# A decoder layer on one core: experts of the first token half in native fp32 beside attention and SSM of the second

## Time and profile before

| | us |
|---|---|
| median of 3 runs | 541.66 |
| lowest, highest | 541.35, 547.73 |
| span of the profiled execution | 542.0 |
| PE busy | 417.3 (77%) |
| DVE busy | 397.2 (73%) |
| ACT busy | 230.3 (42%) |
| POOL busy | 161.0 (30%) |

### The profile page before, as it was taken

The page is one execution under the profiler, slowest core; times in us unless marked ns, Lnnn a source line. Parts: engine busy times, 40 slices in busy tenths (PEclk is TensorE's granted clock), DMA queues, the critical chain, the costliest instruction groups (busy, mean ns, idle before and its releaser), DMA issues.

```text
span 542.0 us, 18523 instructions
## 1 busy us (share of the span) xinstructions
PE 417.3 (77%) x8258; PEld 299.6 (55%) x8258; DVE 397.2 (73%) x542; ACT 230.3 (42%) x434; POOL 161.0 (30%) x118
## 2 busy tenths in 40 slices
PE   1987357887666859867746778749999996999994
PEld 0634146554554445554444443427888875888883
DVE  0545925999989996899984899988785885846434
ACT  1485284553550435544422344304646532344430
POOL 2000743000001000000000000315888875589861
PEclk9996666659867777866676897869999997999998
DMA  8112510250331132211122121510233222323201
GB/s 251 66 24 70 160 24 4 81 133 11 62 96 47 42 96 65 80 42 43 42 81 81 43 79 41 156 46 22 62 86 88 63 74 79 98 79 96 79 1 39
DMA packets 23434, 38.37 MB, mean 71 GB/s; under 512 B 4657, under 2 KB 7483, under 8 KB 23355
## 3 DMA queue, kind: packets, MB, share of 16 engines
q1 hardware_dynamic: 23195, 37.15, 24.3%
q0 software_dynamic: 160, 0.04, 0.1%
HBM read 35.93 MB, written 1.25 MB: 69 GB/s over the span
## 4 chain that ended last, share of the span: by engine, by line
PE 47%; DVE 35%; issue 11%; ACT 4%; DMA 1%; SPq 1%; DVEq 0%; ACTq 0%
PE bank L793 10%; DVE arena_h L1396 8%; PE bank L782 7%; DVE arena_h L1401 4%; PE bank L997 4%; PE bank L998 4%; PE bank L1001 4%; DVE arena_h L1390 4%; PE bank L977 4%; PE bank L978 4%; PE bank L979 4%; PE bank L983 2%; DMA xT<-in_x_t 1%; PE bank L811 1%; DVE u L1351 1%
## 5 line engine op out<-in xcount | busy, mean ns | idle before, releaser
L782 PE MATMUL bank<-arena_h,const 128*128 128x512 f32 x128 | 85.3, 808 | 10.3 <-DVEq L1402 10.2
L719 POOL TENSOR_TENSOR hg_lo<-vkp,hg_hi 128x512 fp32r<-128x512 f32 x50 | 67.8, 1359 | 40.5 <-DVE hg_hi L1617 40.5
L715 POOL TENSOR_TENSOR w_ring<-w_raw,w_ring 128x512 fp32r<-128x512 f32 x16 | 24.2, 1520 | 179.9 <-ACT w_ring L1254 179.9
L1396 DVE TENSOR_TENSOR_SCAN arena_h<-arena_s,arena_h 128x1024 f32<-128x1024 f32 x32 | 73.2, 2288 | 2.9 <-ACT arena_s L1114 1.8
L793 PE MATMUL bank<-vkp,tiles 32*32 32x32 f32 (+1 forms) x3072 | 40.0, 205 | 35.0 <-issue 23.3
L1261 ACT ACTIVATE vkp<-bank,b 128x512 f32<-128x512 f32 x50 | 34.5, 689 | 72.4 <-POOL hg_lo L719 52.0
L1617 DVE CAST hg_hi<-vkp 128x512 fp32r<-128x512 f32 x50 | 33.7, 676 | 38.0 <-PE bank L1001 34.7
L793 PEld LDWEIGHTS bank<-vkp,tiles 32*32 32x32 f32 x3072 | 36.7, 124 | 40.1 <-issue 26.9
L1114 ACT ACTIVATE arena_s<-delta,negA 128x510 f32<-128x510 f32 x64 | 43.1, 713 | 36.8 <-DVEq L1397 36.3
L793 PE MATMUL bank<-qke,tiles 32*32 32x48 f32 (+1 forms) x1984 | 35.3, 233 | 23.5 <-issue 16.7
L782 PEld LDWEIGHTS bank<-arena_h,const 128*128 128x128 f32 x128 | 29.1, 247 | 39.9 <-issue 25.9
(11 more groups left out here) (175 smaller groups left out, 902.3 us busy)
## 6 DMA issues: line engine op xcount, KB each, us to landing
bc<-scr_x SPq DMA_DIRECT2D x32, 512.0 KB, 4.9
raw_ahead<-in_w SPq DMA_DIRECT2D x26, 256.0 KB, 2.7
w_raw<-in_w SPq DMA_DIRECT2D x24, 256.0 KB, 2.7
xT<-in_x_t SPq DMA_DIRECT2D x1, 1024.0 KB, 7.7
xres<-in_x_tok SPq DMA_DIRECT2D x1, 1024.0 KB, 9.7
beta_kc<-scr_b SPq DMA_DIRECT2D x32, 32.0 KB, 1.8
out<-xres SPq DMA_DIRECT2D x8, 128.0 KB, 1.8
wqkvb<-in_wqkvb SPq DMA_DIRECT2D x1, 784.0 KB, 5.6
```

What stands on the lines that cost most here:

```text
L715: pool.tensor_tensor(w[:, 1, :], w_raw[i % RAW][:, :], w[:, 0, :], ALU.subtract).then_inc(s_wlo, 1)
L719: pool.tensor_tensor(hg_lo[i % 2][:, :], hrel[:, i % 2, :], hg_hi[i % 2][:, :], ALU.subtract).then_inc(s_hglo, 1)
L782: mm = pe.matmul(o[:, :], ident, hst[i % NHC][:, GT_ * et:GT_ * et + GT_], start=(n == 0), stop=(n == DS - 1))
L1396: link(dve.tensor_tensor_scan(h, dA[:, i % 2, :], h, 0.0, ALU.mult, ALU.add))
```

## The change

The experts of half 0 become native fp32 products with the weights as loaded (two of 512 columns and four of 256 per tile; no high and low parts), and get buffers of their own (`arena_e`), so that they need only half 0's middle, not the end of attention. Half 1 keeps the fp32r parts; there ACT writes the relu in place in PSUM and makes the high part of the hidden values, DVE the gate product and the low part, POOL only the low part of the weights. Gates go by DMA: a half's gates are transposed, stored to DRAM and broadcast to the rows of each tile (`spread_gates`, four buffers), in place of the selector product. The four largest scores come from max8 and match_replace. Conv, silu and softplus go by token half; softplus's subtractions and `du` move from POOL to DVE. The masked copies of UW move from DVE to ACT. UW, GQ, H and O on PE are cut into two halves each for the planner, whose durations, `BEGIN` and `AHEAD` are new. Waits on the POOL-loaded constants count six loads, b2 among them.

```diff
-BEGIN = {1: ("dve", "solve2"), 3: ("dve", "UW1"), "dt": ("dve", "P3")}
-AHEAD = {("attention", 3): -10, ("experts", 1): -50, ("middle", 0): -10, ("ssm", 0): 30, ("ssm", 1): 10, ("else", 0): 40}
+BEGIN = {1: ("dve", "kn", 0)}
+AHEAD = {"attention0": 25, "attention1": 452, "attention2": -29, "attention3": -46, "ssm0": 27, "ssm1": -40, "middle0": -71, "middle1": -47, "experts0": -46, "experts1": 607, "else": 28}
...
+def prepare(op):
...
+    for i in range(4):
+        conv.append(op("dve", "conv", i, 2.7, [xe[i], *conv[-1:]]))
+        if i % 2:
+            silu.append(op("act", "silu", i // 2, 2.3 if i == 1 else 1.1, [conv[i], *silu]))
...
+    for th in range(NG):
+        p = op("pe", "dt_rows", th, 1.8, [silu[th], p], takes=[("xdbl", th)], ins=8)
...
+        a = op("act", "dt", th, 7.3, [p, nega, *([du[0]] if th else [])], frees=[("dt", th, 0), ("dt", th, 1)])
+        du.append(op("dve", "du", th, 5.2, [a, kept[th]]))
...
+def expert(op, i, split, begin, gst, seq, first):
+
+    th, ft = divmod(i, FT)
+    hid, rel, mul, lo, outs, loads, wlo, grow = seq
+    if th == 0:
+        w = op("sp", "wload", i, .3, [outs.get(i - RAW), loads.get(i - 1), first], lag=3.2)
+        loads[i] = w
+        hid[i] = op("pe", "hid", i, 1.75, [w, *begin, hid.get(i - 1)], takes=[("h", i)], ins=8)
+    else:
...
+        w = op("act", "whi", i, .64, [w, *begin, outs.get(i - RING) if i >= FT + RING else None, ("act", "whi", i - 1) if i > FT else None])
+        wlo[i] = op("pool", "wlo", i, 1.45, [w])
+        hid[i] = op("pe", "hid", i, 1.42, [wlo[i], split, hid.get(i - 1)], takes=[("h", i)], ins=12)
...
         for i in range(FT * th, FT * th + FT):
...
+            expert(op, i, split, chain_end if th else [free], gst, seq, du[1])
...
+        arena_e = sb("arena_e", [P, (RAW + NHR + NGR) * GT_])
+        w_raw = [arena_e[:, GT_ * k:GT_ * k + GT_] for k in range(RAW)]
+        hrel = [arena_e[:, GT_ * k:GT_ * k + GT_] for k in range(RAW, RAW + NHR)]
+        grow = [arena_e[:, GT_ * k:GT_ * k + GT_] for k in range(RAW + NHR, RAW + NHR + NGR)]
...
+            def spread_gates(j):
+                th, m = divmod(j, GATED)
+                if m == 0:
+                    sp.wait_ge(s_gst, 16 * (th + 1))
+                if j >= NGR:
+                    sp.wait_ge(s_mul, muls(FT * ((j - NGR) // GATED) + FREE + (j - NGR) % GATED))
+                for a, b_, e in gate_rows(FREE + m):
+                    sp.dma_start(grow[j % NGR][a:b_, :], scr_g[th, min(e, NX - 1), :].partition_broadcast(b_ - a)).then_inc(s_grow[j % NGR], 16)
...
             def hidden(i):
...
+                if th == 0:
+                    pe.wait_ge(s_wld[i % RAW], 16 * (i // RAW + 1))
+                    if ft == 0:
+                        pe.wait_ge(s_x3T, 2)
+                    for kt in range(KT):
+                        mm = pe.matmul(o[:, :], w_raw[i % RAW][:, P * kt:P * kt + P], xT[:, kt, 0:GT_], start=(kt == 0), stop=(kt == KT - 1))
...
-                k = ("G", i)
-                if ft >= FREE:
-                    filled(k, pe.matmul(fill(k)[:, :], sel[:, P * ft:P * ft + P], gstk[th], start=True, stop=True))
...
+                if th == 0:
...
+                    for tt in range(4):
+                        mm = pe.matmul(out_bank(th, tt), hrel[i % NHR][:, P * tt:P * tt + P], w_raw[i % RAW][:, D:2 * D],
+                                       start=(ft == 0 and tt % 2 == 0), stop=False, skip_group_check=True)
...
                 if name[:2] == "UW":
...
+                    for g in range(HT):
+                        act.activation(tiles[x][TILE_W][:, int(name[2]), :, :, g, :], o[:, :, :, C:2 * C], ACT.Copy,
+                                       scale=head_mask[:, g:g + 1]).then_inc(s_tile_w[x], 1)
...
+            def hidden_hi(i):
+                act.wait_ge(s_mul, muls(i))
+                if i >= FT + 2:
+                    act.wait_ge(s_hguse, i - 1)
+                act.activation(hg_hi[i % 2][:, :], hrel[i % NHR], ACT.Copy).then_inc(s_hghi, 1)
...
+            def softplus(th):
+
+                dve.wait_ge(s_sp, th + 1)
+                c_ = slice(GT_ * th, GT_ * th + GT_)
+                link(dve.tensor_tensor(sp_w, sp_w, sp_z, ALU.subtract))
+                link(dve.tensor_tensor(sp_l, sp_l, sp_w, ALU.subtract))
+                link(dve.tensor_tensor(delta[:, :, c_], delta[:, :, c_], sp_l.rearrange("p (e t) -> p e t", e=2), ALU.add))
+                dve.nop().then_inc(s_delta, 1)
+                dve.wait_ge(s_xkept[th], 16)
+                link(dve.tensor_tensor(du[:, :, c_], delta[:, :, c_], u[:, :, c_], ALU.mult))
...
             def gates(th, part):
...
+                    for tt in range(4):
+                        ins = dve.max(top8[:, tt, :], sc[:, tt, 0:NE])
+                        ins.then_inc(s_dve, 1)
...
+                    for tt in range(4):
+                        ins = dve.match_replace(sc_left[:, tt, :], top8[:, tt, :], sc[:, tt, :], TAKEN)
...
             def hidden_gated(i):
...
+                if ft >= FREE:
+                    dve.wait_ge(s_grow[j % NGR], g_count[j])
                 dve.wait_ge(s_rel, i + 1)
...
+                if th == 0:
+                    dve.tensor_tensor(h, h, grow[j % NGR], ALU.mult).then_inc(s_mul, 1)
+                    return
...
+            def hidden_lo(i):
+                dve.wait_ge(s_hghi, i - FT + 1)
+                dve.tensor_tensor(hg_lo[i % 2][:, :], hrel[i % NHR], hg_hi[i % 2][:, :], ALU.subtract).then_inc(s_hglo, 1)
```

More of the change, by code:

```diff
@@ L76 @@
 BLOCK, FETCH = 256, 3.75
-BEGIN = {1: ("dve", "solve2"), 3: ("dve", "UW1"), "dt": ("dve", "P3")}
-AHEAD = {("attention", 3): -10, ("experts", 1): -50, ("middle", 0): -10, ("ssm", 0): 30, ("ssm", 1): 10, ("else", 0): 40}
[L79 to L83, removed]
+LOWEST = -3.0e38
+TAKEN = -2.0e38
+BEGIN = {1: ("dve", "kn", 0)}
+AHEAD = {"attention0": 25, "attention1": 452, "attention2": -29, "attention3": -46, "ssm0": 27, "ssm1": -40, "middle0": -71, "middle1": -47, "experts0": -46, "experts1": 607, "else": 28}
+SSM = ("decay0", "decay1", "dbu", "scan", "add", "sum", "bc")
+MIDDLE = ("gate", "yT", "ynorm", "x3T", "split", "gst", *(f"gates{part}" for part in range(GATE_PARTS)))
+EXPERTS = ("hid", "relu", "mul", "hi", "lo", "out", "wload", "gload", "whi", "wlo", "b2", "fin", "nst", "nap", "outs")
+OTHER = ("xe", "conv", "silu", "wb", "b", "beta_st", "nega", "dt_rows", "dtlo", "rows", "kept", "zero", "dt", "du", "y_out", "sel", "v")
 def stage(name, i):
     if name in SSM:
-        return "ssm", i // DS
+        return f"ssm{i // DS}"
     if name in MIDDLE:
-        return "middle", i
+        return f"middle{i}"
+    if name == "gload":
+        return f"experts{i // GATED}"
     if name in EXPERTS:
-        return "experts", i // FT
-    return ("else", 0) if name in OTHER else ("attention", i)
+        return f"experts{i // FT if name in EXPERTS[:10] else i}"
+    return "else" if name in OTHER else f"attention{i}"
 class Plan:
@@ L857, in step @@
-                if name[:2] == "GQ":
-                    pe.wait_ge(s_tile_w[x], 2 * n + int(name[2]) + 1)
-                    k = (name, b)
-                    o = fill(k)
-                    for half in range(2):
-                        for c in cs:
-                            at = 2 * C * (CH * half + c % CH)
-                            mm = products(o, slice(at, at + 2 * C), x, TILE_W, half, c, vkp[x][:, half, c, C:W3], True, True)
-                    filled(k, mm)
+                    o = bank[turns[k][0]] if half else fill(k)
@@ new lines, in step @@
+                    for c in cs:
+                        at = 2 * C * (CH * half + c % CH)
+                        mm = products(o, slice(at, at + 2 * C), x, TILE_T, half, c, vkp[x][:, half, c, 0:2 * C], True, True)
+                    if half:
+                        filled(k, mm)
+                if name[0] == "H":
+                    pe.wait_ge(s_uv[x], 2 * n + ch + 1)
+                    o = bank[turns[k][0]] if half else fill(k)
+                    for c in cs:
+                        if c > NREC:
+                            continue
+                        at = C * (CH * half + c % CH)
+                        mm = products(o, slice(at, at + C), x, TILE_KT, half, c, hcn(k_uv[x][:, :])[:, half, c, :],
+                                      half == 0 and c % CH == 0, False)
+                    if half:
+                        filled(k, mm)
@@ L867, in step @@
+                if name[:2] == "GQ":
+                    pe.wait_ge(s_tile_w[x], HT * (2 * n + ch + 1))
+                    o = bank[turns[k][0]] if half else fill(k)
+                    for c in cs:
+                        at = 2 * C * (CH * half + c % CH)
+                        mm = products(o, slice(at, at + 2 * C), x, TILE_W, half, c, vkp[x][:, half, c, C:W3], True, True)
+                    if half:
+                        filled(k, mm)
                 if name[0] == "S":
@@ L1634, in _ @@
                 elif name == "rows":
```

(4 more changed lines are left out.)

729 lines of the change are left out of this document (339 added, 390 removed).

## The result

The changed kernel takes 509.3 us (median of four runs, 505.9 to 510.9) where the kernel before takes 542.1 on the same chip: a ratio of 0.935, 95% interval [0.928, 0.942]. On another chip it came to 509.4 against 542.0, 0.937 [0.930, 0.945]. It is faster, on the side forecast, and 21 us above the 488 predicted, inside the range of 460 to 528. The profiled execution here took 508.0 us, its span is 506.0.

The account below looks back on a forecast made before the run. It took a VectorE-paced stretch of 344 us, then a TensorE-paced one of 171, to bound the kernel. Half 0's tiles through at 405.2, plus 70.5 tiles, 3 gate wait, 2 bias, 7.7 norm and store: 488 us, range 460 to 528.

Parts of the forecast that it names:

- Most signs: First scan step near 45 us, half 0's tiles 212 to 405, clock near 0.9, half 1's tiles 2.8 us apart.
- One sign of being wrong: Between scans, VectorE waits for gate rows or hidden products, its busy share falling below 0.8.
- the likeliest case: Whole kernel: the forecast itself, 477 to 508 us around 488, given chance 0.45.
- (d): Half 0's middle lags by about half the present lag, so tiles start late: 508 to 531 us; chance 0.14.
- (a): Half 0's tiles pace behind VectorE at the low clock: 93.5 us more on TensorE, 582 us; chance 0.05.
- (b): Half 0's tiles end up behind half 1's scan: 570 us, half of them 529; 0.04 slower, 0.07 no change.
- (c): Before half 1's tiles TensorE keeps up and VectorE is last: 476 us, or 456; chance 0.25.
- (e): Weight and gate-row broadcasts bound half 1's tiles: tail 52 us longer, 540 us; within the 0.07 of no change.
- I put its start at 45 us: Start of the first scan step, called 87.79 us in the kernel before: forecast 45 us, bounds 40 and 60.
- The tail: From half 1's first tile: 25 tiles 70.5 us, gate wait 3, bias products 2.0, norm and store 7.7.
- two errors against each other: TensorE beside half 0's tiles: instruction gaps, some 24 us, and clock gain, up to 26, both left out.
- the 10 us put in for norms and adds: VectorE before half 1's scan end: layer norms of batches 2 and 3, half 0's final norm, about +10 us.

Follow-up runs that it names:

- e8: Changed kernel, order only: half 0's tiles held until half 1's y_out and the norms of batches 2 and 3; 553.6 us, 1.014 of the kernel before.
- e2: Changed kernel with half of the fp32 products of half 0's tiles left out; 497.4 us, 0.914 of the kernel before.
- e6: Changed kernel with the 23 gate products of half 0 moved from VectorE to GpSimd; 513.4 us, 0.930 of the kernel before.
- e5: Changed kernel, priorities only: softplus of half 0 ahead of v copies and beta, half 0's gates early; 509.1 us, 0.931 of the kernel before.
- e10: Changed kernel with attention's P, base, H, O in row groups of 64, smaller buffers, priorities anew; 514.2 us, 0.943 of the kernel before.
- e7: Changed kernel with two of four row groups of attention's small products left out, order kept; 477.3 us, 0.873 of the kernel before.

## Why the prediction was right, and where its number was off

**Right in kind.** TensorE last, with VectorE's path ready 15 us before it (forecast 12; both came later than forecast, 403.5 for 393 and 418.8 for 405); tiles beside the scans; the end of half 1's scans at 374 (forecast 375). Most signs came: first half-0 products at 0.92 us each (8 records, four products, in 3.67 us), TensorE without a pause between the halves, tiles of half 1 at 2.9 us (forecast 2.8). One sign of being wrong came too: between half 0's first tile and half 1's read-out VectorE is busy 113.8 of 147.0 us, a share of 0.77 and so below 0.8, since it waits for hidden products:

```profile
226.75:373.70 146.95, 126.18 (x3453) 81.24 (x3454) 113.83 (x148) 55.15 (x122) 0.00 (x0) 0.92 0.31 90
```

It did no harm to the forecast because TensorE was last. e8 shows that the gain is the overlap, e2 and e6 that VectorE does not set the end. The time lies 1 us above the likeliest case (477 to 508), in the range of (d), 508 to 531. But the mechanism of (d), a middle of half 0 that lags, is not what put it there: that middle took 28 us instead of 23. (a), (b), (c) and (e) did not come. Against (a), cold tiles, stands the clock of 0.94 from half 0's first tile on. The Trainium skill (TensorE: Matmul & The Clock Gate, Part 1) says that sustained activity lifts the clock and gaps lower it; the trace agrees, 0.74 with TensorE busy 117 of 175 us, 0.94 with 171 of 192, and 0.85 in e2 with 140 of 175.

**The sum, step by step.** The prediction took the row at 87.79 for the first scan step; it is the first state product, and its stage of 136.2 us is counted from there. So "I put its start at 45 us" is to be held against the first state product, at 51.8 (the bounds were 40 and 60). That is +6.8. From there to the read-out of half 0's scans it took 146.9 against 144 (+2.9), and its middle 28.0 against 23 (+5.0), so the first tile came at 226.8, not 212: the mis-sized terms are these three, the start the largest. From there TensorE took 192.0 us; the sum had 193.2 (-1.2). The tail took 87.2 against 83.2 (+4.0). Together that is 17.6 us before rounding, which leads from 488.4 to the span of 506.0; the time of the profiled run is 2 us above its span and the median 1 us above that. Of the tail's 4 us, 2.0 are half 0's bias products, which stand there too (row at 420.46) and were counted once, and 2.6 are the tiles, 2.92 us each instead of 2.82; the waits, 2.4 us (one is the row at 429.40), are less than the 3 allowed. "28 tiles" in the stretch of 95.5 us is a misreading as well: its 529 records hold the 25 tiles of half 0, the first three hidden parts of half 1 and 37 other products. The sum does not use it.

The first scan was late because of ScalarE's queue, which the prediction left out: softplus of half 0, from 36.3 us on, stood behind the v copies (23.5 to 30.4), beta and the first k (to 36.0), and VectorE was idle 10.6 and 6.8 us before its part of it:

```profile
43.59 1.23 DVE L1420 TENSOR_TENSOR arena_e<-arena_e 128x1024 f32<-128x1024 f32 x1 [6.77 <-ACT arena_e L1121]
```

No run brought the first scan to 45, so what it would give is open. But e5, with its first scan 4 us later and its first tile 6.5 us earlier, ends where the changed kernel does, so neither mark decides the end by itself. The right bound was TensorE's whole account up to half 1's first tile: 324.6 us busy, 56.5 in gaps (line 798 and the sums), 37.6 in named waits.

**Two pairs of errors cancelled.** The forecast took TensorE's other work at 95.7 + 4 us and neither gaps nor gain by clock, as "two errors against each other", 24 and up to 26. Measured: gaps 20.3; busy 171.3, of which tiles 98 (47.4 hidden, 50.5 output), so the rest took 73 instead of 99.7. On VectorE the window up to the end of the stage in which half 1's scan ends in the kernel before:

```profile
0.00:363.30 363.30, 253.86 (x7260) 161.75 (x7260) 280.46 (x353) 156.81 (x319) 34.56 (x24) 0.76 0.26 73
```

and up to the read-out in the changed kernel:

```profile
0.00:373.70 373.70, 279.52 (x7413) 178.51 (x7414) 280.46 (x384) 166.27 (x342) 3.88 (x11) 0.84 0.30 85
```

280.5 in both, not 305. The groups of VectorE in the second window say why:

```profile
L1651 DVE TENSOR_TENSOR arena_e<-arena_e 128x512 f32<-128x512 f32 x12 | 8.2, 692 | 19.2 <-ACT arena_e L1293 17.9 <-DVE arena_h L1460 0.8 <-DVE arena_h L1455 0.4
...
L1508 DVE TENSOR_TENSOR tmp_o<-a_own,tt_s 128x512 f32<-128x512 f32 x4 | 4.1, 1022 | 0.2
...
L1629 DVE MATCH_REPLACE8 sc_left<-top,sc 128x20 f32<-128x20 f32 x4 | 0.6, 163 | 0.0
L1622 DVE MAX8 top<-sc 128x8 f32<-128x16 f32 x4 | 0.4, 164 | 0.0
```

Only 12 of the 23 gate products fall before the read-out (8.2 us, not 15.7); the ranking costs 1.3 us in max8, match_replace and their value loads, not 4; a solve product of 512 elements takes 1.02 us, where it took 1.29 to 1.55 us in the mean before (16 of them, -5.5); and of the 10 us put in for norms and adds 2.5 came before the read-out, the rest behind it. But VectorE also waited more: from the first state product to the read-out it is busy 259.9 of 321.9 us, a share of 0.81 where 0.877 was taken, with 17.9 us of waits on hidden products. So the end at 374 came out right by luck: the work was 24 us less than forecast, and it took longer for its amount.

## What to carry to other kernels

When work of one engine is moved beside another's, forecast the end by the whole account of the engine that becomes last (busy time at the clock it will have, gaps, waits), not by the moment at which the moved work can start: here an earlier start of the tiles (e5) left the end where it was. A wait "for nothing that the profile shows" in front of long runs of small products is here a price of their number; fewer instructions are worth it only if busy time does not rise by as much (39 us of gaps against 34 of busy time in e10).

## What the runs showed of the hardware

**Instruction supply.** 29 gaps before small products come to 54.3 us of TensorE with 6912 such products, 15.3 with 4928 and 1.2 with 3456; those of 1 us or more end 1.2 to 1.6 us after an instruction packet has landed. The Trainium skill (Runtime: NRT & Kernel Launch, Instruction fetch mechanics) says that instructions come in blocks of 16 KiB by a queue of the engine's own, and that the fetch is hidden behind issue. The first half agrees with the trace (63 packets for 1.03 MB, 16 KB each); the second does not hold for runs of such small products, by e7's 31 us, and the measurement decides.

**Row groups.** Half of the row groups left out (e7) took 3456 of 6912 small products away and brought their busy time from 103.7 to 95.2 us (the four groups of that line), so the third and fourth group of 32 rows cost little beside the first two; half as many products of 64 rows (e10) took 37.6 us where 32-row ones took 26.9.
